# A new order of projection, scaling and sums in a fused attention and feed-forward kernel, and the maxima of the two heads taken one by one

## The reference

```
xn  = layernorm(x)
h   = layernorm(xn) * ln_scale + ln_bias
c_q, c_kv = h @ w_down_q.T, h @ w_down_kv.T            # 64 wide each
q, k, v   = c_q @ w_up_q.T, c_kv @ w_up_k.T, c_kv @ w_up_v.T   # 16 heads of 64
q, k      = rope(q), rope(k)
attn      = softmax(q k^T / 8) v  per head;  attn @ w_out.T + xn
y   = relu(xn @ W_fc.T)^2 @ W_proj.T                    # 512 wide inside
s   = (number of spikes of a leaky integrator fed y, 5 steps) / 5
out = x + attention(xn) + s
```

## Time and profile before

| | us |
|---|---|
| median of 3 runs | 1337.35 (1335.43 to 1348.48) |
| the profiled execution, its own time | 1334.07 |
| its span | 1332.3 |
| granted TensorE clock, mean | 0.96 |

### The profile page before, as it was taken

How to read it: one execution, slowest core, us unless ns; L and a number is a source line. 1 busy time by engine, 2 the same in 40 slices (tenths; PEclk the granted TensorE clock), 3 DMA queues, 4 the chain that set the end, 5 groups by cost and what they waited for, 6 DMA issues and landing times.

```text
span 1332.3 us, 25712 instructions
## 1 busy us (share of the span) xinstructions
PE 1093.0 (82%) x6880; PEld 753.1 (57%) x6880; DVE 984.1 (74%) x1350; ACT 837.0 (63%) x2945; POOL 804.2 (60%) x837
## 2 busy tenths in 40 slices
PE   3678888889788888788888888888888888788886
PEld 2446555556555655556555555555556656556654
DVE  3677788777787777777777787677778777777772
ACT  2666666666666666665666665566666666666650
POOL 3567556566656557656667656566566566656550
PEclk9899999989999999999999999999999999999998
DMA  4466676676576565675665675665676666676562
GB/s 147 118 181 157 158 190 171 165 177 162 157 185 164 161 175 153 166 180 145 179 175 157 167 185 155 162 178 143 167 191 160 171 177 163 160 181 170 160 166 62
DMA packets 93273, 217.87 MB, mean 164 GB/s; under 512 B 22464, under 2 KB 43200, under 8 KB 93120
## 3 DMA queue, kind: packets, MB, share of 16 engines
q1 hardware_dynamic: 72768, 150.45, 48.8%
q10 hardware_dynamic: 20480, 67.13, 13.4%
HBM read 7.77 MB, written 4.19 MB: 9 GB/s over the span
## 4 chain that ended last, share of the span: by engine, by line
PE 32%; issue 28%; POOL 20%; DVE 12%; ACT 4%; SPq 1%; DVEq 1%; DMA 1%; POOLq 0%; ACTq 0%
PE ps_s L300 12%; PE ps_u L318 9%; POOL partner L740 6%; POOL qk L743 6%; PE ps_b L396 5%; DVE neg_max L605 4%; POOL relu_sb L780 4%; PE ps_a L369 4%; DVE turned L614 3%; ACT prob L482 3%; POOL rstd L755 2%; DVE u_n L628 1%; DVE qk L600 1%; PE ps_qk L291 1%; PE ps_qk L290 1%
## 5 line engine op out<-in xcount | busy, mean ns | idle before, releaser
L482 ACT ACTIVATE prob<-ps_s,neg_max 128x256 f32<-128x256 f32 x1024 | 472.0, 476 | 392.8 <-DVE neg_max L605 356.5
L740 POOL TENSOR_TENSOR partner<-partner,rope_sb 128x512 f32<-128x512 f32 x256 | 325.7, 1272 | 437.5 <-DMA partner<-raw 437.3
L605 DVE TENSOR_REDUCE neg_max<-ps_s 128x4 f32<-128x1024 f32 x256 | 312.5, 1221 | 216.9 <-PE ps_s L300 216.6
L318 PE MATMUL ps_u<-gathered,ckv 128*64 128x256 f32 x2048 | 288.4, 403 | 88.9 <-ACT rden_t L553 60.3
L300 PE MATMUL ps_s<-qk 64*128 64x256 f32 x2048 | 307.5, 421 | 45.7 <-POOL qk L743 45.7
L743 POOL TENSOR_TENSOR qk<-qk,partner 128x512 f32<-128x512 f32 x256 | 325.4, 1271 | 20.1
L614 DVE STREAM_TRANSPOSE turned<-prob 128x1024 f32<-128x1024 f32 x256 | 314.4, 1228 | 1.3 <-ACT prob L482 0.4
L300 PEld LDWEIGHTS ps_s<-qk 64*128 64x128 f32 x2048 | 185.1, 195 | 162.8 <-issue 78.1
L318 PEld LDWEIGHTS ps_u<-gathered,ckv 128*64 128x64 f32 x2048 | 133.3, 140 | 164.4 <-issue 105.4
L482 ACT ACTIVATION_READ_ACCUMULATOR prob<-ps_s,neg_max 128x1 f32 x1024 | 212.1, 207 | 0.0
L600 DVE TENSOR_TENSOR qk<-ps_qk,rope_sb 128x512 f32<-128x512 f32 x256 | 171.2, 669 | 49.3 <-PE ps_qk L291 48.4
(11 more groups left out here) (57 smaller groups left out, 887.0 us busy)
## 6 DMA issues: line engine op xcount, KB each, us to landing
gathered<-turned SPq DMA_DIRECT2D x1024, 128.0 KB, 2.4
partner<-raw ACTq DMA_DIRECT2D x256, 256.0 KB, 2.5
x_sb<-in_x SPq DMA_DIRECT2D x32, 128.0 KB, 2.4
resid<-xn_sb SPq DMA_DIRECT2D x32, 128.0 KB, 2.0
out<-out_sb SPq DMA_DIRECT2D x32, 128.0 KB, 1.8
turned<-in_wup SPq DMA_DIRECT2D x2, 512.0 KB, 6.1
rope_sb<-in_rope SPq DMA_DIRECT2D x1, 512.0 KB, 7.1
turned<-in_wo_t SPq DMA_DIRECT2D x1, 512.0 KB, 8.4
```

Source lines behind the costliest of these rows:

```text
L318: last = nc.tensor.matmul(ps_u[h * L:(h + 1) * L, 0, :], ckv[:, (s // PAIRS) % 2, kt, :], gathered[:, (s // GROUP) % 2, :, s % GROUP, h, k ...
L482: last = nc.scalar.activation(prob[:, s % 2, :, h, :, t, :].rearrange("p j k c -> p k j c"), ps_s[:, s % 2, h, t, :].rearrange("p (k j c) ...
L605: nc.vector.tensor_reduce(neg_max[:, s % 2, :, :], ps_s[:, s % 2, :, :, :], AXIS_X, ALU.max, negate=True).then_inc(max_ready, 1)
L740: nc.gpsimd.tensor_tensor(other, other, sin_sb, ALU.mult).then_inc(sin_ready, 1)
```

## The change

The maximum of each head is its own instruction with its own semaphore, and ACT waits for each before that head's two exponentials. On PE `project` stands directly behind `scores`, ahead of the extras. On DVE `rotate` and the extras up to `finish` stand ahead of `turn`. On ACT `copy_projected` and `exchange` stand directly behind the exponentials, ahead of the extras and of `copy_u`. The transposed inverse sums and the transposed final sum move from `ps_u` to `ps_b`; the four chunks of scaling move from steps 7, 0, 1, 2 to steps 0 to 3, the four output sums from 3 to 6 to 4, 5, 6, 6, the transpose of the inverse sums from step 6 to step 7, and their copy from step 6 to the start of step 0. `weigh_latents` in steps 6 and 7 loses its waits for that copy and for `finish`. On POOL `inverse_std` goes from ahead of the rotation in step 1 to behind it in step 0, the squares from steps 0, 1 to 1, 2, `split_sums` from 2 to 5. `invert_sums` goes from step 1 to 4.

```diff
@@ tensor: weigh_latents
                 pe.wait_ge(u_evac, done(g - 1))
-                if s % PAIRS == 6:
-                    pe.wait_ge(rt_evac, done(i * UNROLL + s // PAIRS))
-                elif s % PAIRS == 7 and not outside(i * UNROLL + s // PAIRS - 1, B):
-                    pe.wait_ge(final_done, done(i * UNROLL + s // PAIRS - 1))
@@ tensor: transpose_rden, broadcast_rden, transpose_sum
-                pe.wait_ge(u_evac, done(PAIRS * b + 5))
+                pe.wait_ge(acc_ready, done(b - 1))
...
-                if c == 0:
-                    pe.wait_ge(acc_ready, done(b - 1))
-                else:
+                if c > 0:
                     pe.wait_ge(u_norm, done(CHUNKS * b + c - 1))
@@ tensor: extras
-                    if p < 3:
-                        broadcast_rden(b - 1, p + 1)
-                    elif p < 7:
-                        attention_out(b - 1, p - 3)
+                    if p < 4:
+                        broadcast_rden(b - 1, p)
+                    elif p < 6:
+                        attention_out(b - 1, p - 4)
+                    elif p == 6:
+                        attention_out(b - 1, 2)
+                        attention_out(b - 1, 3)
+                    elif p == 7:
+                        transpose_sum(b - 1)
                 if p == 7:
                     if not outside(b, B):
-                        broadcast_rden(b, 0)
-                    if not outside(b - 1, B):
-                        transpose_sum(b - 1)
+                        transpose_rden(b)
@@ tensor: step
-                extras(b, b0, p)
                 if not outside(g + LEAD["project"], STEPS):
                     project(g + LEAD["project"], s + LEAD["project"], i)
+                extras(b, b0, p)
@@ scalar: exponentials
-                act.wait_ge(max_ready, done(g))
...
                 for h in range(2):
+                    act.wait_ge(max_ready[h], done(g))
@@ scalar: copy_rden
                 act.wait_ge(rt_ready, done(b))
+                act.wait_ge(final_done, done(b - 1))
@@ scalar: step
+                if p == 0 and not outside(b - 1, B):
+                    copy_rden(b - 1)
                 if not outside(g + LEAD["scores"], STEPS):
                     exponentials(g + LEAD["scores"], s + LEAD["scores"], i)
+                if not outside(g + LEAD["project"], STEPS):
+                    copy_projected(g + LEAD["project"], s + LEAD["project"], i)
+                if (s + LEAD["project"]) % 2 == 1 and not outside(g + LEAD["project"], STEPS):
+                    exchange(g + LEAD["project"], s + LEAD["project"])
...
                 if not outside(g, STEPS):
                     copy_u(g, s, i)
@@ vector: row_max
-                nc.vector.tensor_reduce(neg_max[:, s % 2, :, :], ps_s[:, s % 2, :, :, :], AXIS_X, ALU.max,
-                                        negate=True).then_inc(max_ready, 1)
+                for h in range(2):
+                    nc.vector.tensor_reduce(neg_max[:, s % 2, h, :], ps_s[:, s % 2, h, :, :], AXIS_X, ALU.max,
+                                            negate=True).then_inc(max_ready[h], 1)
@@ vector: step, the order in a step afterwards
+   add_spikes (p == 7); row_max; rotate; normalise_u (p < 4); moments_of (0), split_latents (3),
+   invert_sums (4), finish (7); turn; integrate (5 and 6)
@@ gpsimd: step, the order in a step afterwards
+   add_rotated; inverse_std (0); square (1 and 2); residual (3); split_sums (5)
```

More of the change, by code:

```diff
@@ L135, in build @@
         ps_s = pb("ps_s", [P, 2, 2, TT, S])
-        ps_u = pb("ps_u", [P, 2, S])
+        ps_u = pb("ps_u", [P, 512])
         ps_a = pb("ps_a", [P, 512])
@@ L154, in build @@
         rope_done = sem("rope_done")
-        s_ready, max_ready, exp_done = sem("s_ready"), sem("max_ready"), sem("exp_done")
+        s_ready, exp_done = sem("s_ready"), sem("exp_done")
+        max_ready = [sem(f"max_ready{h}") for h in range(2)]
         rden_ready, rden_hi, rden_split = sem("rden_ready"), sem("rden_hi"), sem("rden_split")
@@ L318, in weigh_latents @@
                         last = nc.tensor.matmul(
[L319 removed]
+                            ps_u[h * L:(h + 1) * L, 0:S], ckv[:, (s // PAIRS) % 2, kt, :],
                             gathered[:, (s // GROUP) % 2, :, s % GROUP, h, kt, :, :].rearrange("p i t r -> p t i r"),
@@ L375, in transpose_rden @@
                 pe.wait_ge(rden_split, done(b))
-                pe.wait_ge(u_evac, done(PAIRS * b + 5))
+                pe.wait_ge(acc_ready, done(b - 1))
                 for t in range(TT):
-                    last = nc.tensor.transpose(ps_u[:, 1, t * P:(t + 1) * P], rden_hl[:, t, :].bitcast(F32), ident_sb[:, :])
+                    last = nc.tensor.transpose(ps_b[:, S + t * P:S + (t + 1) * P], rden_hl[:, t, :].bitcast(F32), ident_sb[:, :])
                 last.then_inc(rt_ready, 1)
@@ L401, in transpose_sum @@
                 pe.wait_ge(acc_ready, done(b))
[L402 to L405, removed]
                 for t in range(TT):
-                    last = nc.tensor.transpose(ps_u[:, 0, t * D:(t + 1) * D], acc_t[:, t * P:(t + 1) * P], ident_sb[:, :])
+                    last = nc.tensor.transpose(ps_b[:, t * D:(t + 1) * D], acc_t[:, t * P:(t + 1) * P], ident_sb[:, :])
                 last.then_inc(fin_ready, 1)
@@ L416, in value_by_output @@
                             rows = slice(h * DH, (h + 1) * DH)
-                            last = nc.tensor.matmul((ps_u[:, :, :].rearrange("p j s -> p (j s)"), ps_b)[half][h * L:(h + 1) * L, j * D:(j + 1) * D],
+                            last = nc.tensor.matmul((ps_u, ps_b)[half][h * L:(h + 1) * L, j * D:(j + 1) * D],
                                                     wv_sb[rows, pair, :], wo_sb[rows, pair, :],
@@ L509, in copy_u @@
                     act.wait_ge(u_norm, done(CHUNKS * (b - 1) + pair // 2))
-                nc.scalar.copy(u_raw[:, pair, :], ps_u[:, 0, :]).then_inc(u_evac, 1)
+                nc.scalar.copy(u_raw[:, pair, :], ps_u[:, 0:S]).then_inc(u_evac, 1)
             def normalise(n, par, which, i):
@@ L550, in copy_rden @@
                 act.wait_ge(rt_ready, done(b))
+                act.wait_ge(final_done, done(b - 1))
                 if not outside(b - 1, B):
                     act.wait_ge(bc_ready, done(CHUNKS * (b - 1) + CHUNKS - 1))
-                nc.scalar.copy(rden_t[:, :], ps_u[:, 1, :]).then_inc(rt_evac, 1)
+                nc.scalar.copy(rden_t[:, :], ps_b[:, S:2 * S]).then_inc(rt_evac, 1)
             def prologue():
@@ L670, in finish @@
                 dve.wait_ge(fin_ready, done(b))
+                if not outside(b + 1, B):
+                    dve.wait_ge(rt_ready, done(b + 1))
                 dve.wait_ge(copied[par], 16 * (i + 1))
```

60 lines of the change are left out of this document (24 added, 36 removed).

## The result

The changed kernel takes 1371.47 us (median of 4 runs, 1369.37 to 1372.68), the kernel before 1338.58 beside it. The ratio is 1.0231 with a 95% interval of 1.0176 to 1.0286: 2.3% slower, where 3% faster was forecast. It is the forecast's rival (c) by its mechanism.

The account below looks back on a forecast made before the run. No engine was taken as the bound; PE's waits were. PE work 31.8 plus stalls 5.8 gave 37.6 us; 0.2 for rounding and 0.6 for falls made 38.4 against 39.7, over 31 elements 1296 us; range 1264 to 1330.

Parts of the forecast that it names:

- rival (c): Clock falls twice in each element, behind step 2 and steps 4 and 5: element 40.9 us, kernel 1371 us; chance 0.09.
- Waits of steps 6 and 7: weigh_latents on PE no longer waits for rden_t and finish, nothing takes their place: gain 2.8 us in the element read.
- The walk at full clock: One element traced through the new lists: PE work 31.8 us plus stalls 5.8, together 37.6 against 38.50.
- Falls of the clock ... I take half of them, 0.6: Falls cost 1.2 to 2.2 us in elements having them; denser stretches around step 2 halve them, adding 0.6 us.
- The sign of being wrong that the prediction named: Among the signs that would make the prediction wrong: the count of clock falls goes up.
- Split maximum: On DVE two instructions of 0.61 to 0.67 us replace one of 1.22; ACT may start 0.53 us sooner where it waits.
- Rival (d): The split does nothing because ACT is late in every step: element 38.9 us, 1311 us; upper edge of the forecast's 0.58.
- `turn` behind the split: DVE's turn behind the waiting split delays step 4's maxima, so project in step 5 waits 1.5 us, eating half the gain.
- Exchange: Issued earlier on ACT, step 1's starts 2 us sooner; with a 4.3 us landing wait POOL is in time for step 4.
- rival (b): Exchange lands 1.2 us later than 4.3, delaying step 4's scores: element 39.6 us, 1325 to 1336 us; chance 0.15.

Follow-up runs that it names:

- a_fill: Changed kernel with throwaway products in TensorE's two long stalls, 16 in step 4 and 12 in step 2: 1288.5 us, ratio 0.9634 to the kernel before.
- a_fill4: Changed kernel with only the stall of step 4 filled, by 16 throwaway products: 1315.5 us, ratio 0.9798 to the kernel before.
- v2: Changed kernel with lead_latents behind exponentials, turn ahead of the split, copy_u ahead of odd-step exchange, input transposes behind weigh_latents: 1209.61 us, ratio 0.9051 to before.
- experiment 5: Kernel before with 12 throwaway products in its stall of step 2, ahead of the wait for normalised inputs: 1346.01 us, ratio 1.0119.

## Why the prediction was wrong

**Waits of steps 6 and 7: right.** They are gone and nothing took their place in those steps: steps 6 and 7 together take 8.54 us (667.93 to 676.47) against 10.82 before. Of the 2.8 us waited there 2.3 are gained, and step 6 now holds two output sums where it had one.

**The walk at full clock: right in its sum, not in step 4.** It gave 37.6, with 0.2 for what it rounds off 37.8; `a_fill` measured 38.05. The stalls foretold were 1.1 (step 0, measured 1.02) and 1.9 (step 2, 2.30). In step 4 a step of the working failed. It put the wait for the split latents at `ffn_out`, 1.1 us, and a second one of 1.5 at `project` in step 5. The trace shows one wait, at `project` in step 4, 2.73 us. `project` works 12 pairs ahead, so step 4 begins the latents of the element after next, and `project` now stands ahead of the output sums and of `ffn_out`, which before had filled that time. 1.1 and 1.5 are nearly 2.7, so the element's length at full clock came out right, in this part by luck; but the idle time came in one piece.

**"Falls of the clock ... I take half of them, 0.6": this step failed**, and decided the sign. Measured: two in each element, 2.95 us, so five times the term; 58 falls in 31 gaps, where before had 26. The sign of being wrong that the prediction named, a count of falls that goes up, came. The reason given for fewer was that the stretches around step 2 had become denser. Against it stands the one piece of 2.73 us in step 4, where the walk had two smaller ones. In step 2 the idle time hardly grew: 2.30 us in one piece, where before had 2.05 in two, 1.20 and, which the prediction's reading left out, 0.85 ahead of the broadcast:

```profile
672.98 0.51 PE L388 MATMUL ps_b<-rden_t,sel_sb 128*128 128x256 f32 x2 [0.85 <-DVE u_n L628]
```

37.8 + 3.1 = 40.9 was rival (c)'s sum, with a chance of 0.09; 41.0 was measured. The mechanism was right; that the number fits so well is luck, since 37.8 was 0.25 too low and 3.1 was 0.15 too high, and its second fall was placed behind two stalls that came as one. Its condition, 1.6 falls an element, is reckoned at 1.2 us a fall; at the measured 1.5 the loss begins at 1.1 falls. `a_fill` and `a_fill4` show the price by experiment. The Trainium skill (TensorE: Matmul & The Clock Gate, What's actually happening) states that the clock follows how busy PE has been recently. This case agrees: throwaway work alone gave the 83 us back.

**Split maximum.** The cost was nearly right: 0.683 us each, just above the bounds of 0.61 and 0.67; since the two overlap a little, the pair takes 1.29 us where one took 1.22. The Trainium skill's fixed term (VectorE: DVE Perf Modes, The TRN2 errata), with its estimate of 0.69 us, is nearest. At full clock the split gave 1.1 us an element, as much as twice the 0.53 us; at which steps was not shown. Rival (d), by which it does nothing, is out at full clock.

**`turn` behind the split: wrong.** "A new wait, four links long, and it eats half": the edit of `turn` alone gave 1 us, and `project` in step 5 did not wait. The costly link was ScalarE's order, named in the same paragraph.

**Exchange: held.** The late landing of rival (b) didn't come. From the end of step 1's issue (686.00 and 1.36 us) to POOL's start at 691.10 it is 3.74 us, where the walk had 4.3 and rival (b) 5.5, and PE's wait for POOL before the scores is 9.8 us over the span, where it was 45.7.

## What to carry to other kernels

A stall of TensorE is to be priced with what comes behind it: here 2.7 us in one piece was followed by slow products that cost 1.6 us more, and 1.0 us at the same place by none. The prediction had the length of the idle time nearly right and the sign wrong, because it expected fewer falls than before. So when an order is changed, look for the waiting instruction that now stands first on TensorE with its filling work behind it, and put the work ahead of the wait; `v2` got most of its 61 us by moving four transposes behind the products that had stood behind them. A fall can also be free: where the next instruction waits for another engine anyway, as in step 4 of the kernel before, full speed ahead of it only lengthens the wait (experiment 5). Before a change is judged by its time, compare elements at full clock: this one was 2.3% slower and held a schedule that, with a few orders mended, is 11% faster than before.

## What was not expected of the hardware

The changed kernel has elements of 41.0 us with the split maximum and two falls, and elements of 41.0 us without the split and with one fall. A stall of 2.30 us in step 2 brought a fall in the former, one of 2.19 us brought none in the latter, and in `a_fill4` the same stall of step 2 brought one in 15 gaps of 31. So the length of the idle time alone doesn't say whether the clock falls, and the runs here don't settle what else does. Filling a stall with products that nobody reads made a kernel 6% faster, which no count of busy time would suggest: PE's busy time in two elements is 71.69 us with it and 70.03 in the changed kernel.
